# Twelve products of each projection tile spread over eight steps of the attention pipeline instead of six

## The reference

```python
x = x + 0.5 * ffn(layernorm(x))        # layernorm(x) @ ternary(weight).T + bias
x = x + attention(layernorm(x))        # below
x = x + 0.5 * ffn(layernorm(x))

q = rope((x @ w_q.T).reshape(B, T, 16, 32).transpose(0, 2, 1, 3))
k = rope((x @ w_k.T).reshape(B, T, 16, 32).transpose(0, 2, 1, 3))
v =      (x @ w_v.T).reshape(B, T, 16, 32).transpose(0, 2, 1, 3)
scores = where(mask, q @ k.T / sqrt(32), -inf)   # causal, in blocks of 64 tokens
x_out  = (softmax(scores) @ v).reshape(B, T, 512) @ w_o.T
```

## Time and profile before

| | us |
|---|---|
| median of 3 runs | 701.97 (700.91 to 702.2) |
| the profiled execution | 700.48 |
| its span, first to last instruction | 698.7 |
| PE busy | 594.4 (85%) |
| DVE busy | 427.1 (61%) |
| ACT busy | 294.4 (42%) |
| POOL busy | 117.4 (17%) |

### The profile page before, as it was taken

The page is one execution under the profiler, slowest core; times in us unless marked ns, Lnnn a source line. Parts: engine busy times, 40 slices in busy tenths (PEclk is TensorE's granted clock), DMA queues, the critical chain, the costliest instruction groups (busy, mean ns, idle before and its releaser), DMA issues.

```text
span 698.7 us, 9869 instructions
## 1 busy us (share of the span) xinstructions
PE 594.4 (85%) x3586; PEld 221.7 (32%) x3586; DVE 427.1 (61%) x878; ACT 294.4 (42%) x597; POOL 117.4 (17%) x104
## 2 busy tenths in 40 slices
PE   0676978799999999998758687879999999999885
PEld 0433433232332322234324333333233222222342
DVE  5996389776777771015576755976767777200472
ACT  1721211245556677743305121113645657684241
POOL 2301422122132000001010142221222301010100
PEclk9997999899999999999879899989999999999998
DMA  9420422212112000000410033222122110000002
GB/s 327 160 26 23 136 69 93 88 46 79 58 52 87 1 2 1 1 1 1 180 61 0 1 111 115 68 71 89 47 69 69 46 47 2 1 1 1 1 27 93
DMA packets 34893, 41.16 MB, mean 59 GB/s; under 512 B 3012, under 2 KB 27716, under 8 KB 34846
## 3 DMA queue, kind: packets, MB, share of 16 engines
q1 hardware_dynamic: 31962, 36.23, 16.1%
q10 hardware_dynamic: 2884, 4.30, 1.7%
HBM read 23.62 MB, written 16.78 MB: 58 GB/s over the span
## 4 chain that ended last, share of the span: by engine, by line
PE 66%; DVE 23%; ACT 5%; issue 3%; DMA 1%; POOL 1%; SPq 0%; ACTq 0%; DVEq 0%; POOLq 0%
PE bank L705 12%; PE bank L677 10%; PE bank L765 10%; PE bank L756 10%; PE bank L689 8%; PE bank L648 6%; PE bank L640 6%; DVE rot L575 5%; DVE rmax L558 5%; PE bank L733 3%; DVE stats L476 2%; DVE t L568 2%; ACT big L375 2%; ACT xh L373 2%; DMA vs<-in_L_attn_x_dram 1%
## 5 line engine op out<-in xcount | busy, mean ns | idle before, releaser
L558 DVE TENSOR_REDUCE rmax<-bank 128x1 f32<-128x512 f32 (+3 forms) x384 | 200.2, 554 | 94.5 <-PE bank L689 90.7
L404 ACT ACTIVATE big<-bank 128x512 f32<-128x512 f32 (+3 forms) x384 | 175.9, 488 | 147.9 <-PE bank L677 145.1
L689 PE MATMUL bank<-kst,qst 104*128 104x512 f16 (+3 forms) x384 | 125.8, 336 | 23.6 <-DVE rmax L558 22.6
L677 PE MATMUL bank<-qst,kst 106*128 106x512 f16 (+3 forms) x384 | 120.8, 332 | 2.3 <-ACT big L404 1.2
L756 PE MATMUL bank<-big,ones 128*32 128x512 f32 (+3 forms) x768 | 81.8, 498 | 0.9 <-ACT cf L424 0.9
L765 PE MATMUL bank<-big,vs 128*32 128x512 f32 (+3 forms) x768 | 81.8, 498 | 0.0
L677 PEld LDWEIGHTS bank<-qst,kst 106*128 106x128 f16 x384 | 34.6, 96 | 143.1 <-ACT big L404 99.2
L334 POOL TENSOR_TENSOR t<-t,rot 128x512 f32<-128x512 f32 x32 | 40.5, 1266 | 199.9 <-DVE rot L575 199.9
L705 PE MATMUL bank<-xh,wh 128*128 128x512 f16 x128 | 42.0, 426 | 18.0 <-DVE xl L519 13.6
L689 PEld LDWEIGHTS bank<-kst,qst 104*128 104x128 f16 x384 | 38.1, 99 | 59.7 <-DVE rmax L558 21.7
L344 POOL TENSOR_TENSOR cl<-cf,ch 128x512 f16<-128x512 f32 x16 | 18.5, 1158 | 202.1 <-ACT ch L430 202.1
(11 more groups left out here) (76 smaller groups left out, 575.1 us busy)
## 6 DMA issues: line engine op xcount, KB each, us to landing
spread<-rhl SPq DMA_DIRECT2D x32, 256.0 KB, 2.2
qst<-spread SPq DMA_DIRECT2D x16, 384.0 KB, 3.6
kst<-spread SPq DMA_DIRECT2D x16, 384.0 KB, 3.8
vs<-in_L_attn_x_dram SPq DMA_DIRECT2D x4, 1024.0 KB, 6.7
spread<-rhl SPq DMA_DIRECT2D x32, 128.0 KB, 2.1
out_dram<-xs ACTq DMA_DIRECT2D x16, 256.0 KB, 2.0
xs<-in_L_ffn_weight_dram SPq DMA_DIRECT2D x1, 1024.0 KB, 8.4
kst<-in_L_attn_w_q_dram SPq DMA_DIRECT2D x1, 1024.0 KB, 12.6
```

Of the source, the lines that this page charges most:

```text
L404: nc.scalar.activation(probs[:, st % P_PLACES, h, 0:n], pb[u % 2][:, 0:n], ACT.Exp, scale=EXP_SCALE).then_inc(s_eb, 1)
L558: nc.vector.tensor_reduce(rmax[:, at:at + 1], pa[u % 3][:, 0:n], AX.X, ALU.max, negate=True).then_inc(s_max, 1)
L677: nc.tensor.matmul(pb[u % 2][:, 0:n], kst[0:ROWS_B, g % SETS, h, j * P:(j + 1) * P], qst[0:ROWS_B, g % SETS, h, q0:q0 + n], start=True, st ...
L689: nc.tensor.matmul(pa[u % 3][:, 0:n], qst[0:ROWS_A, g % SETS, h, i * P:(i + 1) * P], kst[0:ROWS_A, g % SETS, h, half * HALF:half * HALF + ...
```

## The change

`SLOTS` lists which of a tile's twelve products each step issues: two in steps 0, 1, 4 and 5 of the window, one in steps 2, 3, 6 and 7. Before, steps 0 to 5 issued two each. The number of products, their order among themselves and their operands stay. The last product moves from step 5 to step 7 of the window, and by `proj_after` everything that hangs on it moves two steps later: `t` and `rot1` from step 6 to 8, `rot2` from 7 to 9, POOL's from 8 and 0 to 10 and 2, ACT's from 11 to 1 of the next window, SP's two issues from 1 and 4 to 3 and 6. The order of these among SP's and POOL's own instructions stays as it was.

```diff
+SLOTS = [(0, 1), (2, 3), (4,), (5,), (6, 7), (8, 9), (10,), (11,)]
@@
-            if 0 <= g < GROUPS and r % A_UNITS < 6:
+            if 0 <= g < GROUPS and r % A_UNITS < len(SLOTS):
                 return g, r // A_UNITS, r % A_UNITS
@@
-            return u[:2] if u and u[2] == 5 else None
+            return u[:2] if u and u[2] == len(SLOTS) - 1 else None
@@
-                        for n in (2 * i, 2 * i + 1):
+                        for n in SLOTS[i]:
                             a, cc = divmod(n, CC)
...
-                        if i == 5:
+                        if i == len(SLOTS) - 1:
                             last.then_inc(s_proj, 1)
                             evacuated += 1
```

## The result

The changed kernel takes 725.57 us (median of 4 runs, 721.87 to 731.13) against 701.83 for the kernel before (4 runs, 700.91 to 702.2). The ratio is 1.0347, with a 95% interval of 1.0269 to 1.0425. So it is slower, as forecast, but by 24 us and not by 14, and the median lies above the range. The runs of the changed kernel lie 9 us apart, those of before 1.3 us. The profiled execution took 728.34 us, with a span of 726.6.

The account below looks back on a forecast made before the run. PE was taken to bound steps 114 to 191, DVE steps 66 to 89. Terms 6.6 + 1.0 - 0.6 = 7.0 us a batch row, 14.0 for both, gave 714.5 profiled, 716.0 as median; range 706 to 723.

Parts of the forecast that it names:

- The mechanism of the wait: Window steps 6 to 12: rot2 now ends DVE's order after R8; T waits in step 10, delaying everything behind it.
- the wide window: Window of step 138 (186 alike): T at 5.73 us after A6, A12 at 7.49 against 5.70, net +1.36 us.
- the narrow one: Window of step 126 (174 alike), B has 128 columns: T at 4.98 us, A12 at 6.10, net +0.67 us.
- my signs of being wrong: Windows of the pipeline: T does not wait, A6 to A12 keeps its length, or new half-speed stretches appear.
- The sum of the wait: Steps 114 to 191, seven PE-bound windows: T's wait less the spreading's gain adds 6.6 us a batch row.
- the half-clock term: Steps 108 to 113 at half the clock: two products fewer save 0.86 us.
- Steps 54 to 113: DVE-bound windows +1.0 us, windows 90 and 102 with the half-clock steps -0.6 us a batch row.
- The DVE-bound windows: Windows of steps 66 and 78: DVE stalls as A12 comes later, 0.5 us each, 1.0 in all.
- The late stack: Rival: tile 3's first reader waits, 0.7 us at step 58, about 1 at step 106; 718, chance 0.05.
- this start: Steps 0 to 58: tile 3's later chain offset by fewer products at half clock; taken as 0, bounds 0 to +0.7.
- The clock rival: Rival: longer idle time before T causes two or three more half-clock drops, adding 5 to 7 us: 722, chance 0.2.
- The rival on the other side: Rival: DVE's chain is done when PE reaches T, only the spreading's gain is left: 695 us, chance 0.06.

Follow-up runs that it names:

- the section on ACT's copy: Changed kernel with DVE's t, rot1 and rot2 a step earlier (694.3 us), with ACT's copy at lag 4 instead of 6: 694.39 us, ratio 0.9894.
- the short filler: Changed kernel with six further unread products in front of T, only in the windows of steps 114 to 186: 715.35 us, ratio 1.019.
- the filler in every window: Changed kernel with six further unread products in front of T in the windows of steps 114 to 234: 727.68 us.

## Why the prediction was wrong

*The mechanism of the wait was right.* T waits for `rot2`, and the chain starts with R8 behind A8. In the wide window T was forecast at 5.73 us after A6 and came at 5.85 (171.13 - 165.28), A12 at 7.49 and came at 7.60. In the narrow one T was forecast at 4.98 and came at 5.10, A12 at 6.10 and came at 6.21. All four are 0.1 us late. R8 started where I had put it, 2.51 and 1.76 us after A6. The chain behind it took 3.28 us in both windows where I had taken 3.16. I had let both reduces overlap what follows, but only R8 did (`t` starts 0.48 us after it), while `rot2` starts 0.72 us after R9.

*The step that failed is the clock.* The sum has no term for new half-speed stretches. I had put them into a rival of its own, with a chance of 0.2, because PE had never been below full clock in that stage, "where T already waits". That row could not carry it: the waits there were at most 0.33 us in front of T, and the ones I forecast (1.8 and 2.2 us) were more than five times as long. The forecast itself created the condition and then used the old clock. It measured 13.6 us in the profiled execution, more than the 5 to 7 that the rival had. I had priced two or three drops in all and there were nine in this stage alone. The price of one, 1.5 us, was below my 2.4. (Rows 10, which I named beside this rival, show the 3.33 us of idle time only; in the trace the clock is at half behind it, from 91.64 to 95.05 us.) Nor does one trace show that the kernel before is free of them: 13 runs of it beside the first experiments lie between 699.56 us (granted clock 0.956) and 704.85 (0.949), and the profiles of two variants of it, with at most 1.45 us in front of T, have three such spells (two in the one with only DVE moved, one in the one with only T moved). New stretches at half speed were also the last of my signs of being wrong; the others that I gave came as forecast or nearly (T's idle time 1.40 to 2.29 us, A146 to A148 2.36 us).

*The sum of the wait* was 6.6 us a batch row for steps 114 to 192 and measured 7.8 with the clock at full. A third of the difference is a count: I took the 0.43 us gain off seven windows, but only six sets of steps 0 to 5 lie in this stage. The seventh was already in the half-clock term. The rest is mainly the chain's 0.12 us in the wide and narrow windows, a gain of only 0.30 in place of 0.43 in steps 0 to 5 behind the two narrow ones, and a mean that was too low for the window of 150. The windows by the full-clock kernel (A6 to the next A6, against before) were +0.5 (114), +0.9 (126, 174), +1.5 (138), +1.3 (150) and +0.8 (162), and +1.9 for A6 to A12 of 186. The forecast's 0.5, 0.67, 1.36, 1.0 and 1.0 are of that size.

*Steps 54 to 113* were forecast at +0.4 us a batch row (1.0 - 0.6) and measured +1.0 and +0.8 (50.82 and 50.60 before, 51.83 and 51.44 after; here the two rows of before are not alike to the hundredth). The DVE-bound windows came at the size worked out: A66 to A90 took 17.44 us before and 18.29 after, 0.43 a window where I had taken 0.5. The stretch behind them was forecast at -0.6 and measured -0.1 and -0.5 (A90 to A114). Steps 54 to 65, taken as 0, measured +0.3 and +0.5.

*The late stack* showed at step 58, as the rival had it, and once more elsewhere. A57 to A58 grew by 0.62 and 0.79 us (3.71 and 3.54 to 4.33), of which the steps up to 66 gave 0.43 and 0.35 back. The other place was not step 106 but step 202, for 0.67 us and 0.82 us in the two rows (192 to 204). I had written that the later groups keep "some us", without a row. The kernel with ACT's copy two steps earlier shows that ACT's place is the cause at step 202.

*Put together,* against the span of before the profiled execution has 29.2 us more in steps 114 to 192 (15.6 wait, 13.6 clock), 1.9 in 54 to 113 and 1.5 in 192 to 203: 32.6, of which 27.9 show in the time. The other 4.7 us came back where no A runs. Most of it is inside the pipelines: from the first P to A of step 54 it takes 27.69 and 27.72 us in place of 29.69 and 29.32, 3.6 us less, while I had put this start at 0. The cause is probably ACT's later copy, which no longer holds up line 383 (see the section on ACT's copy); it was not taken apart further. The end is 1.0 us shorter, where the code is the same. So against the 14.0 of the sum, the clock added 13.6 us and undersized terms about 5, of which 4.7 were hidden by this. With the short filler, and so without the spells of this stage, the profiled execution takes 713.15 us, close to the 714.5 of the sum; that closeness is partly luck, two errors of about 5 us that cancel.

*The range* reached to 723 and left out the clock's full size. The clock rival's own time of 722 was its likeliest value and not its end. One drop for each window with a long wait, 14 of them at the 2.4 us that I had for one, would have been 34 us.

*The rival on the other side* (695 if T does not wait) is close to what the kernel with DVE one step earlier takes: 694.3. The number agrees better than its parts. The rival counted 0.43 us in six stretches, 2.6 us a row, and 0.86 at half the clock. Steps 114 to 192 gave 1.0 a row, since T still waits in the narrow windows and the wide ones got 0.43 longer; steps 54 to 113 gave 1.9 and 1.5, steps 192 to 203 took 0.7 and 0.9, and the start of the pipelines gave 1.2 and 1.3.

## What to carry to other kernels

When follow-up work moves as a block, look for the one instruction that did not move and now stands ahead of its producer in an in-order queue. Its wait is paid by everything behind it, and moving it, or the producer, by one step can be worth more than the edit itself: 684.6, 694.3 and 725.6 us differ only in the step numbers of T, DVE's three products and ACT's copy, by one or two each. Such moves do not add up: two that gain nothing alone gain 9 us together (692.3), because each only shifts the wait to the other's place. When a forecast puts new idle time in front of TensorE, price the clock with that new idle time in mind, not with the clock of the old trace. A cheap test of whether a loss is wait or clock is to fill the gap with products that nobody reads; where there is no gap, they cost their full length.

## What the runs showed of the hardware

TensorE fell to half speed in a stage in which it was still 87% busy by the profile (83.91 of 96.63 us). The gaps in front of T there were 1.4 to 2.3 us long, one in each 14 us. The filler shows that this idle time is the cause: with 1.3 us of work in such a gap, and part of it still idle (0.10 to 1.00 us), there was no spell at half speed in 181 us.

The length of a gap alone did not decide. In the changed kernel a spell began behind or in the window of 114 (2.29 us) and that of 162 (2.09) in both batch rows, in those of 126 and 174 (1.99) in one row each, in that of 150 (1.56) in one row, and none in those of 138 and 186 (1.40). In the kernel with only the follow-up steps moved, the same 1.99 us were followed by a spell in the window of 162 and by none in those of 126 and 174. Gaps of 1.45 us in the window of 114 were followed by one in two rows out of six (three kernels). With only T moved, a spell came in one row with no idle time in front of T at all, behind three waits of 0.39, 0.61 and 0.75 us within 5 us.

A piece of 3.4 us at half speed cost 1.5 us here, and a run had several. That fits the spread of the runs, 9 us here and 0.6 with the filler in every window.
